# A decoder kernel on one core: triangular solve in two 16-step blocks joined by matmuls, and causal filters as Toeplitz products through DRAM

## The reference

```python
A = einsum('bhncd,bhned->bhnce', kbc, kc)            # 32x32 per chunk
T = eye + tril(A, -1)
inv = solve_triangular(T, eye, lower=True, unit_diagonal=True)
u = inv @ vc ; w = inv @ kbc                         # then a scan over the chunks
paths = [_fir(v_direct, f) for f in (fir_w3, fir_w7, fir_w15, fir_w31)] + [delta_out]
router_in = concat([hidden_states] + paths)          # mixing weights of the five paths
```

## Time and profile before

| what | us |
|---|---|
| runs: low, median, high | 1011.01, 1013.28, 1014.31 |
| the profiled execution's own time | 1015.0 |
| its span, first to last instruction | 1013.2 |
| TensorE busy | 940.2 |
| VectorE busy | 731.4 |
| ScalarE busy | 653.3 |
| GpSimd busy | 334.9 |
| mean granted TensorE clock | 0.958 of 2.4 GHz |

### The profile page before, as it was taken

The page is one execution under the profiler, slowest core; times in us unless marked ns, Lnnn a source line. Parts: engine busy times, 40 slices in busy tenths (PEclk is TensorE's granted clock), DMA queues, the critical chain, the costliest instruction groups (busy, mean ns, idle before and its releaser), DMA issues.

```text
span 1013.2 us, 22026 instructions
## 1 busy us (share of the span) xinstructions
PE 940.2 (93%) x7958; PEld 601.1 (59%) x7958; DVE 731.4 (72%) x2866; ACT 653.3 (64%) x1531; POOL 334.9 (33%) x720
## 2 busy tenths in 40 slices
PE   7988999999995879999999999999977889999996
PEld 4777675645432546668776756565334555777675
DVE  2565769899998876857563688777899996764624
ACT  4498989886553235677987778566543246778743
POOL 3766323633322011537322422141240022433222
PEclk9799999999997699999999999999986999999998
DMA  9400000121353221100000000103543210000001
GB/s 314 164 1 1 1 2 11 43 53 43 95 121 65 58 54 32 43 11 22 1 13 1 1 12 22 45 9 84 115 106 74 62 36 11 11 12 1 11 1 32
DMA packets 77692, 45.44 MB, mean 45 GB/s; under 512 B 53008, under 2 KB 68880, under 8 KB 77328
## 3 DMA queue, kind: packets, MB, share of 16 engines
q1 hardware_dynamic: 77584, 44.04, 16.5%
HBM read 33.01 MB, written 11.01 MB: 43 GB/s over the span
## 4 chain that ended last, share of the span: by engine, by line
PE 69%; DVE 16%; ACT 7%; DMA 2%; POOL 2%; issue 2%; SPq 1%; ACTq 0%; POOLq 0%; DVEq 0%
PE psum L1102 7%; PE psum L995 7%; PE psum L921 6%; PE psum L559 6%; PE psum L1092 3%; PE psum L860 3%; PE psum L832 3%; PE psum L834 3%; DVE pool L1583 3%; PE psum L1086 3%; PE psum L1088 3%; DVE sol_t L1588 3%; PE psum L568 2%; ACT pool L1818 2%; ACT pool L2023 2%
## 5 line engine op out<-in xcount | busy, mean ns | idle before, releaser
L1804 ACT ACTIVATE pool<-psum 128x512 f32<-128x512 f32 x144 | 83.3, 596 | 58.1 <-PE psum L921 27.9
L1818 ACT ACTIVATE pool<-pool,small 128x128 f32<-128x128 f32 x224 | 91.6, 484 | 38.3 <-POOL small L2185 38.1
L559 PE MATMUL psum<-sb_const,pool 128*128 128x128 f32 x672 | 99.1, 282 | 9.6 <-ACT pool L1818 2.8
L921 PE MATMUL psum<-pool,firw 128*32 128x512 f32 (+7 forms) x960 | 106.4, 578 | 0.1
L2180 POOL TENSOR_SCALAR small<-small 128x4 f32<-128x4 f32 x88 | 22.2, 252 | 249.9 <-DVE small L1174 247.8
L559 PEld LDWEIGHTS psum<-sb_const,pool 128*128 128x128 f32 x672 | 78.3, 145 | 38.3 <-issue 19.0
L2183 POOL TENSOR_TENSOR small<-small,minus_half 128x4 f32<-128x4 f32 x88 | 92.3, 1049 | 7.3
L995 PE MATMUL psum<-pool,sb_l1a 128*128 128x512 f32 x192 | 92.1, 632 | 2.1 <-ACT pool L1804 2.1
L1102 PEld LDWEIGHTS psum<-sb_l1f,pool 128*128 128x128 f32 x640 | 78.3, 192 | 15.6 <-issue 13.9
L1102 PE MATMUL psum<-sb_l1f,pool 128*128 128x128 f32 x640 | 83.5, 278 | 0.0
L1405 DVE TENSOR_TENSOR pool<-pool,psum 128x512 f32<-128x512 f32 x80 | 52.7, 681 | 38.7 <-ACT pool L2090 16.6
(11 more groups left out here) (428 smaller groups left out, 2146.4 us busy)
## 6 DMA issues: line engine op xcount, KB each, us to landing
pool<-scratch_kk SPq DMA_DIRECT2D x18, 256.0 KB, 3.7
pool<-in_cF SPq DMA_DIRECT2D x16, 256.0 KB, 3.3
scratch_kk<-pool SPq DMA_DIRECT2D x10, 256.0 KB, 2.6
pool<-in_xF SPq DMA_DIRECT2D x8, 256.0 KB, 6.1
pool<-in_x SPq DMA_DIRECT2D x8, 256.0 KB, 6.2
scratch_xt<-pool SPq DMA_DIRECT2D x8, 256.0 KB, 2.0
pool<-scratch_xt SPq DMA_DIRECT2D x8, 256.0 KB, 3.2
scratch_kk<-pool SPq DMA_DIRECT2D x32, 64.0 KB, 2.0
```

What stands on the lines that cost most here:

```text
L559: m = e.transpose(f.ap[:, part(b)], src[:, part(b)], ident)
L921: m = e.matmul(b4(f.ap)[32 * c:32 * c + 32, :, 4 * kg:], firw[:, col, :], vsh[:, c, :, 0:P - 4 * kg], start=n == 0, stop=n == len(kgs) - 1)
L1804: e.activation(slot(g, i), f.ap, ACT.Copy).then_inc(f.emptied, 1)
L1818: m = e.activation(dst[:, part(b)], src[:, part(b)], ACT.Identity, bias=v["nm"][:, b:b + 1], scale=v["r"][:, b:b + 1])
```

## The change

**Filters.** v is now taken in token order (slot 2, as `b_vT` leaves it), written to a DRAM buffer with 32 zero rows ahead of each sequence, 64 features at a time, and read back as overlapping windows of 48 tokens (one for every 16 tokens; 32 per group), features innermost. Partitions 0 to 47 hold the windows of features 0 to 63, partitions 64 to 111 those of 64 to 127. Per feature one matmul multiplies its 48x32 windows (stationary, every 64th element of a row) by a 48x64 Toeplitz matrix of all four filters for 16 output tokens (moving). These matrices are built once, by the new steps `s_t` and `s_u`, by DMAs: 64 that place the taps, 48 that lay one lag each (512 rows of 16 elements), 2 that load. `b_fir` has two steps of 64 matmuls. Its four results are copied out of PSUM, written to DRAM in runs of 16 elements (`b_fs.0`, `.1`) and read back by feature in four DMAs (`b_fl`). `b_ez`, `firw` and the edge zeroing go.

**Solve.** The two diagonal 16x16 blocks of each triangle are solved at once, on two partitions: `b_x` has 15 steps in place of 31, `nm, ni = k + 1, 15 - k`. GpSimd lays the unit rows (`b_sol`) and a unit block (`b_rs`). The block below the diagonal comes from TensorE: `b_i1` (four transposes), `b_i2` (64 matmuls with 16-row operands, into four banks) and `b_i3` (64 matmuls), with six ScalarE copies between them. The turned inverses need no reordering on the way back (`b_xt` reads 2 KB rows).

**Walk and tiles.** `ORDER` is new from the first to the last entry, with the new steps in it. `ones` is kept as one column, four pieces used once land in slot 14 of set 0, a 512-column constant is not loaded any more; the constants arrive in 7 more DMAs. `sol_t`, `idx` and `idx2` move into other tiles.

The diff, without `ORDER` and with the lesser hunks left out:

```diff
+CB = CH // 2
...
+TB, NBLK = 16, P // 16
+NLAG = TB + CH
+ONCE = {"cmask": 0, "bo": 1, "ce_bo": 2, "ebias": 3}
+UNUSED = ("unit_rows",)
+KEPT = {"ones": 1}
...
+    def windows(g):
+        return slot(g, 8, 4).rearrange("p (n c) -> p n c", c=HALF)
+
+    MOVED = {"v": 2, "windows": 10, "sums": 14, "paths": 18}
+
+    def path(g):
+        return sem(f"path{g % NA}"), 16
+
+    def moved(own, g, what):
+        own.wait_ge(sem(f"path{g % NA}"), 16 * (g // NA * MOVED["paths"] + MOVED[what]))
+
+    def blocks(g):
+
+        both = slot(g, 12, 2)
+        return both[:, 0:3 * CB * CB].rearrange("p (m i) -> p m i", i=3 * CB), both[:, 3 * CB * CB:].rearrange("p (j i) -> p j i", i=CB)
+
+    def by_chunk_row(g):
+        return hd(slot(g, 12))
...
+        def s_t(g, k):
+
+            o.wait_ge(sem("zeros_laid"), 1)
+            zeros = flat(toeplitz[:, 0:CH, :])
+            e.dma_start(lags, zeros[:, 0:4 * HALF]).then_inc(sem("toeplitz_laid"), 16)
+            e.dma_start(padded.rearrange("g r b t c -> (g r b) (t c)")[:, 0:CH * HALF], zeros[0:NG * 2 * GB]).then_inc(
+                sem("toeplitz_laid"), 16)
+            o.wait_ge(sem("toeplitz_laid"), 32)
+            first = cols["once_l1"]["fir"][0]
+            for f, k in enumerate(FIRS):
+                kg, n = FIR_GROUPS.index((f, 0)), (k + 3) // 4
+                for s, c in itertools.product(range(4), range(4)):
+                    at = HALF * f + TB - 1
+                    src = dram["once_l1"][CH * s:CH * s + CH, first + 4 * kg:first + 4 * (kg + n)].rearrange("p (k c) -> c p k", c=4)
+                    dst = lags[CH * c:CH * c + CH, at:at + 4 * n].rearrange("p (k s) -> s p k", s=4)
+                    e.dma_start(dst[s], src[c], allow_slow_non_contiguous=True).then_inc(sem("toeplitz_laid"), 16)
+            o.wait_ge(sem("toeplitz_laid"), 32 + 16 * 16 * len(FIRS))
+            by_filter = lags.rearrange("c (f z) -> (c f) z", z=HALF)
+            for lag in range(NLAG):
+                lo = NLAG - 1 - lag
+                e.dma_start(toeplitz_rows[lag], by_filter[:, lo:lo + TB]).then_inc(sem("toeplitz_laid"), 16)
+
+        def s_u(g, k):
+            o.wait_ge(sem("toeplitz_laid"), 32 + 16 * 16 * len(FIRS) + 16 * NLAG)
+            for r in range(2):
+                rows = toeplitz_rows[:, 4 * HALF * r:4 * HALF * r + 4 * HALF, :].rearrange("p m t -> p (m t)")
+                e.dma_start(flat(toeplitz[HALF * r:HALF * r + NLAG]), rows).then_inc(sem("toeplitz_in"), 16)
+
         def b_sh(g, k):
-            a = g % NA
-            vsh = slot(g, 8, 4).rearrange("p (c m) -> p c m", c=4)
-            kept = dram["xt"][g].rearrange("q (h m) -> (q h) m", h=2)
-            o.wait_ge(sem("v_made"), g + 1)
+            f = fill("b_vT", g)
+            o.wait_ge(f.emptied, f.n)
             upper_half(o, g)
-            e.dma_start(kept, slot(g, 5)).then_inc(sem(f"v_out{a}"), 16)
-            o.wait_ge(sem(f"v_out{a}"), 16 * (g // NA + 1))
-            for s in range(4):
-                e.dma_start(vsh[32 * s:32 * s + 32, :, s:],
-                            kept.rearrange("(c p) m -> p c m", c=4)[:, :, 0:GT - s]).then_inc(sem(f"shifted{a}"), 16)
+            for r in range(2):
+                e.dma_start(padded[g, r, :, CH:, :].rearrange("b t c -> t b c"),
+                            b4(slot(g, 2))[:, :, HALF * r:HALF * r + HALF]).then_inc(*path(g))
+            moved(o, g, "v")
+            for r, b in itertools.product(range(2), range(GB)):
+                at = padded[g, r, b, CH + TB - NLAG:CH + TB - NLAG + 1]
+                src = bass.AP(padded.tensor, at.offset, [[HALF, NLAG], [TB * HALF, NBLK], [1, HALF]])
+                e.dma_start(windows(g)[HALF * r:HALF * r + NLAG, NBLK * b:NBLK * b + NBLK], src).then_inc(*path(g))
+
+        def b_fs(g, k):
+            for r in range(2):
+                f = fill("b_fir", g, f"r{r}", k)
+                o.wait_ge(f.emptied, f.n)
+                dst = paths[g, 2 * r + k].rearrange("n p t -> p n t")
+                e.dma_start(dst, slot(g, 3 + 2 * r + k).rearrange("p (n t) -> p n t", t=TB)).then_inc(*path(g))
+
+        def b_fl(g, k):
+            moved(o, g, "sums")
+            by_channel = paths[g].rearrange("r (u f) (j n) t -> j (r u) f (n t)", f=4, j=4)
+            for j in range(4):
+                e.dma_start(slot(g, 3, 4)[j:P:4].rearrange("p (f m) -> p f m", f=4), by_channel[j]).then_inc(*path(g))
...
-            for h in range(2):
-                e.dma_start(slot(g, 13, 2)[64 * h:64 * h + 64], dram["kk"][g]).then_inc(*chunks(g))
+            for d in range(2):
+                d_ = slice(CB * d, CB * d + CB)
+                src = dram["kk"][g].rearrange("r (j i) -> r j i", i=CH)[:, d_, d_]
+                e.dma_start(blocks(g)[1][HALF * d:HALF * d + HALF], src).then_inc(*chunks(g))
 
         def b_xo(g, k):
             a = g % NA
-            x = slot(g, 12).rearrange("p (m i) -> p m i", i=CH)
+            by_row = dram["xt"][g].rearrange("a b -> (a b)").rearrange("(m r i) -> r m i", r=4 * NP, i=CH)
             o.wait_ge(sem("solved"), g + 1)
-            for h in range(2):
-                dst = dram["xt"][g].rearrange("q (m h i) -> h q m i", h=2, i=CH)[h]
-                e.dma_start(dst, x[64 * h:64 * h + 64]).then_inc(*chunks(g))
+            for d in range(2):
+                lo = CB * (1 - d)
+                e.dma_start(by_row[:, CB * d:CB * d + CB, :], blocks(g)[0][HALF * d:HALF * d + HALF, :, lo:lo + CH]).then_inc(*chunks(g))
 
         def b_xt(g, k):
             a = g % NA
             chunked(o, g, "inverses")
-            by_head = dram["xt"][g].rearrange("(h n) (m i) -> h m n i", h=NH, i=CH)
+            by_row = dram["xt"][g].rearrange("a b -> (a b)").rearrange("(m h n) -> h m n", h=NH, m=CH)
             for h in range(NH):
-                e.dma_start(slot(g, 13)[CH * h:CH * h + CH].rearrange("m (n i) -> m n i", i=CH), by_head[h]).then_inc(*chunks(g))
+                e.dma_start(slot(g, 12)[CH * h:CH * h + CH], by_row[h]).then_inc(*chunks(g))
...
-            o.wait_ge(made, MADE["s_b2"])
-            o.wait_ge(sem("edge_zeroed"), 3 * g + 3)
-            o.wait_ge(sem(f"shifted{g % NA}"), 64 * (g // NA + 1))
-            f = begin("b_fir", g, "s", k)
-            vsh = slot(g, 8, 4).rearrange("p (c b t) -> p c b t", c=4, b=GB)
-            kgs = [kg for ff, kg in FIR_GROUPS if ff == k]
-            for n, kg in enumerate(kgs):
-                for c in range(4):
-                    col = FIR_GROUPS.index((k, kg)) * 4 + c
-                    m = e.matmul(b4(f.ap)[32 * c:32 * c + 32, :, 4 * kg:], firw[:, col, :],
-                                 vsh[:, c, :, 0:P - 4 * kg], start=n == 0, stop=n == len(kgs) - 1)
-            m.then_inc(f.filled, 1)
+            o.wait_ge(sem("toeplitz_in"), 32)
+            moved(o, g, "windows")
+            halves = [begin("b_fir", g, f"r{r}", k) for r in range(2)]
+            for u, j, r in itertools.product(range(8), range(4), range(2)):
+                c, r_, j_ = CH * k + 4 * u + j, slice(HALF * r, HALF * r + NLAG), slice(CH * j, CH * j + CH)
+                m = e.matmul(halves[r].ap[j_, HALF * u:HALF * u + HALF], windows(g)[r_, :, c], toeplitz[r_, c, :],
+                             start=True, stop=True)
+                if u == 7 and j == 3:
+                    m.then_inc(halves[r].filled, 1)
...
+        def b_i1(g, k):
+            chunked(o, g, "turned")
+            turn(begin("b_i1", g), slot(g, 12))
+
+        def b_i2(g, k):
+
+            got("b_i1", g)
+            kkt = slot(g, 8, 4).rearrange("p (q t) -> p q t", q=NP)
+            for c in range(4):
+                f, r_ = begin("b_i2", g, f"c{c}"), slice(CH * c, CH * c + CB)
+                for b in range(GB):
+                    for h in range(NH):
+                        m = e.matmul(f.ap[CH * h:CH * h + CH, CB * b:CB * b + CB], kkt[r_, h * GB + b, CH * c:CH * c + CH],
+                                     small[g]["turned"][r_, b * NH + h, :], start=True, stop=True)
+                m.then_inc(f.filled, 1)
+
+        def b_i3(g, k):
+            for c in range(4):
+                got("b_i2", g, f"c{c}")
+            o.wait_ge(sem("unit_beside"), g + 1)
+            f = begin("b_i3", g)
+            for n in range(NP):
+                for h in range(NH):
+                    h_ = slice(CH * h, CH * h + CH)
+                    m = e.matmul(f.ap[h_, CB * n:CB * n + CB], hd(slot(g, 14))[h_, n, :], by_chunk_row(g)[h_, n, CB:],
+                                 start=True, stop=True)
+            m.then_inc(f.filled, 1)
...
-            a = slot(g, 13, 2).rearrange("p (j i) -> p j i", i=CH)
-            x = slot(g, 12).rearrange("p (m i) -> p m i", i=CH)
+            x, a = blocks(g)
+            x = x[:, :, CB:2 * CB]
             k, second = divmod(k, 2)
-            nm, ni = k // 2 + 1, CH - 1 - k
+            nm, ni = k + 1, CB - 1 - k
             tmp = small[g]["sol_t"][:, 0:nm * ni].rearrange("p (m i) -> p m i", m=nm)
             if k == 0 and not second:
```

(54 more changed lines are left out.)

278 lines of the change are left out of this document (151 added, 127 removed).

## The result

Four runs of the changed kernel took 1048.42 to 1054.34 us, median 1049.86; the kernel before took 1013.48 beside them. The ratio is 1.0375, interval 1.0345 to 1.0404. The forecast was 960. The profiled execution took 1054.34 us, its span is 1052.5.

The account below looks back on a forecast made before the run. TensorE was taken to bound the kernel, with VectorE nearly as busy in the two passes. TensorE -39, gaps -20, DMA waits +5 and start +1 gave -53: 962 us profiled, 960 median, range 945 to 975 (chance 0.56).

Parts of the forecast that it names:

- Gaps, −20: In the two passes, half of TensorE's 40.3 us of gaps would go: -20 us.
- Rival 1: Passes stay bound by the dependent chain, gaps take back the gain and bring 1.2 GHz: 980 to 1005 us, chance 0.20.
- Clock: TensorE's granted clock, noted at 0.85 and 0.88 in parts of the passes; given no term in the sum.
- Filters, TensorE: New filter matmuls: 2048 instructions at 19 ns, 39 us in place of 106.4, saving 67 us (16 to 81).
- Solve, TensorE: Added block products b_i2 and b_i3: 2048 instructions at 12 ns, 25 us; b_i1's transposes 3.5 more.
- VectorE −77: VectorE's busy time falls by 77 us through the shorter solve, about 38 per pass, leaving it far from binding.
- DMA queue: Added DMAs, mostly hidden: waits add 5 us in all; queue below 30% busy, a b_fs DMA landing in 4 to 7 us.
- rival 2: 64-byte b_fs packets choke the DMA queue, deciding from about 27 ns each; at 50 ns, 1050 us; chance 0.09.
- Start: Building the matrices in s_t and s_u is hidden; seven more constant DMAs cost 1 us, between 0 and 3.
- Rival 3: Filters' strided weight load not hidden: 44 ns and more per instruction, TensorE +12 us, about 1010 us; chance 0.05.
- The slow rival: Same as rival 2: short b_fs packets at 50 ns hold up later groups' solves, 1050 us, chance 0.09.
- three signs of being wrong: Filter instructions over 40 ns; b_ag or b_xo over 10 us to land; passes staying 225 and 210 us, TensorE idle 60.

Follow-up runs that it names:

- wide4: Changed kernel with b_fir, b_i2 and b_i3 in a quarter of the instructions, four times the moving columns each (other results): 993.63 us, 0.9804 of the kernel before.
- warm: Changed kernel with 184 extra bf16 matmuls ahead of b_i3, b_u and b_p to fill TensorE's waits: 1063.17 us, 1.049 of the kernel before.
- long_runs: Changed kernel with b_fs writing in runs of 2 KB, so filtered paths arrive in wrong order: 1047.31 us, 1.033 of the kernel before.

## Why the prediction was wrong, step by step

The forecast was 962 us for the profiled execution, 1054 was measured, 92 more. TensorE's busy time makes about 30 of them (−9.4 us where −39 was forecast) and its idle time the other 62 or so (121.7 us in place of 73.0, +49, where −20 + 5 + 1 = −14 was forecast).

- **Gaps, −20**: this is the step that failed most. The forecast let half of the 40.3 us of gaps in the passes go. TensorE's idle time in the whole passes went from 44 us to 82. The "issue" pauses ahead of the three new groups are 24.8 us of that; without these pauses (`wide4`) 65 us are left, and their cause was not found. The solve is shorter and VectorE freer (156.3 and 133.7 us busy in the passes), as forecast, but VectorE now waits 46.3 us for L1087 (`b_u`) and 32.4 for L1045 (`b_p`), where it waited 2.0 and 7.0 for the same products before:

```profile
L1609 DVE COPY pool<-psum 32x128 f32<-32x128 f32 x64 | 18.6, 291 | 3.3 <-PE psum L963 2.0
L1603 DVE TENSOR_TENSOR pool<-pool,psum 128x128 f32<-128x128 f32 x24 | 6.8, 285 | 7.4 <-PE psum L949 7.0
```

  Rival 1 named the mechanism (bursts of tiny matmuls, gaps, 1.2 GHz) and ended it at 1005; it was the right story, with the sign wrong. It took the gaps as not recovered; they nearly doubled.
- **Clock**: the second step that failed, left out of the sum as if it cost nothing. The parts that the change touches came out as forecast: filters 33.0 us for 106.4, block products 28.6, all transposes with `b_i1` among them 106.7 for 99.1, together −37 for −39. But TensorE's busy time fell by 9.4 only: the other matmuls, the same in both kernels, take 28 us more, L1028 27.3 us where L932 took 19.8. The granted clock is at 1.2 GHz for 17% of the span in place of 8%, and in the windows of 25 us from 325 and 775 wholly or nearly so (0.50, 0.51). Time at the low clock is (1 − 0.917) x 2 x 1052 = 175 us, before 85 us; on a TensorE some 70% busy there the 90 us more are, as an estimate, 90 x 0.7 / 2, about 30 us of busy time. The low clock goes with the pauses and the idle time: with a quarter of the instructions the mean came back to 0.942. As a remedy by itself it failed (`warm`), though it did give back the 30 us of busy time.
- **Filters, TensorE**: 39 us forecast, 33.0 busy at 16 ns each. **Solve, TensorE**: 25 forecast, 28.6. Both were right as busy time, and had no term for the 11.9 and 19.3 us of idle time ahead. They were priced from bursts of 32 instructions, which seldom meet the end of a block; the steps come in bursts of 128 and 256, which always do. A hint of it stood in the trace of the kernel before, where `b_u` as a whole took 15 ns an instruction, not the 12 of its best burst, with 3.8 us of "issue" ahead:

```profile
L963 PE MATMUL psum<-pool 32*32 32x32 f32 x1024 | 15.7, 204 | 16.2 <-DVE pool L1603 11.6 <-issue 3.8 <-ACT pool L2023 0.5
```

  Removing three quarters of the 4096 instructions gave back 56 us (18 ns each), removing half 38 (19 ns each). In `wide4` a good half of that is busy time and the rest idle time.
- **VectorE −77**: measured −64. In the passes it fell by 34 and 43 us, and they did not get shorter.
- **Copies, ScalarE** 668.3 for 668 forecast. **GpSimd** +8 for up to +24. **DMA queue** 31.7% for under 30, a `b_fs` DMA landing in 8.2 us (median) for 4 to 7, and `long_runs` gained 2.5 us. If the two DMAs of a step share those 8.2 us, their 8192 packets take about 16 ns each per engine, under the 27 from which rival 2 was to decide. **Start**: +1 forecast, 6.4. **Rival 3**, the strided weight load: the filters' 16 ns an instruction are those of `b_i3`, whose weights have no stride, so it did not come.
- **The slow rival** (packets at 50 ns, 1050) met the measured time by its number and not by its cause: luck.
- **What I had asked of the profile**: of the three signs of being wrong one came, the passes kept their 225 and 210 us with TensorE idle for 82 (I had named 60). The other two did not: filter instructions took 16 ns, not over 40, and `b_ag` and `b_xo` landed in 2.3 and 3.4 us (medians), not over 10.

## To carry to other kernels

Price a small matmul by the instruction and not by its columns, and by the length of the burst that it comes in: some 12 to 16 ns of busy time each here, and 31 where a burst of hundreds ran ahead of the supply of instructions. Leave room in the sum for TensorE's clock: 28 us here went to matmuls that the change had not touched. Before adding thousands of them on the path of a dependent chain, look for a form with fewer: four times the columns in a quarter of the instructions was 56 us here. Let neighbouring matmuls of few rows take turns on different parts of the array, and don't test half of a change in another's hand-written order.

## What the runs showed of the hardware that was not expected

- TensorE's instructions come in blocks of 256 (16.4 KB packets); a run of small matmuls paused up to 3.0 us between blocks and went on 1.2 to 1.6 us after the packet had landed; where a pause followed a block at once, the two took 4.0 us.
- Instructions of matmuls with 32 rows and 128 columns of weights took 97 ns each with four matmuls in a row on the same rows (and PSUM bank), 35.5 on four different ones in turn; on the same rows but 32 other columns each (`b_i2`) 12.
- A bf16 matmul of 16 columns cost 11 ns, an f32 instruction of the same shape 12 to 16, and an f32 matmul is two of them: halving precision paid through the count.
